# Two selective-scan layers on one core: the step products move from GpSimd to VectorE, the second output projection is cut into pieces inside the next image's loop, and TensorE adds products of zeros

## The reference

```
xc = silu(conv3x3(x @ W_in))
xs = the points of xc in 4 orders, forward and backward          # 8 scans in layer 0
delta = softplus(dt @ W_dt + b);   A = -exp(A_log)
h = exp(delta * A) * h + (delta * u) * B;   y = sum_n h_n * C_n   # for each point, state n = 0..15
y = layer_norm(sum over scans) * silu(z);   out = y @ W_out
```

## Time and profile before

| | |
|---|---|
| median of 3 runs | 15351.98 us (15345.07 to 15356.31) |
| the profiled execution, its own time | 15355.73 us |
| its span | 15353.9 us |
| granted clock over the span | 0.898 |
| VectorE busy | 13974.8 us, 91% |
| GpSimd busy | 13679.9 us, 89% |
| TensorE busy | 11962.6 us, 78% |
| ScalarE busy | 10343.2 us, 67% |

### The profile page before, as it was taken

How to read it: one execution, slowest core, us unless ns; L and a number is a source line. 1 busy time by engine, 2 the same in 40 slices (tenths; PEclk the granted TensorE clock), 3 DMA queues, 4 the chain that set the end, 5 groups by cost and what they waited for, 6 DMA issues and landing times.

```text
span 15353.9 us, 137291 instructions
## 1 busy us (share of the span) xinstructions
PE 11962.6 (78%) x45056; PEld 6538.9 (43%) x45056; DVE 13974.8 (91%) x8019; ACT 10343.2 (67%) x14003; POOL 13679.9 (89%) x5828
## 2 busy tenths in 40 slices
PE   6777877778777787777877778777787777877778
PEld 4543345433444334443345433444334443345433
DVE  8998989989899899998999989999898998989988
ACT  5666766667666676666766667666676666766667
POOL 7997989979899798997889978899789997899978
PEclk8898988989889898898988989889898898988989
DMA  5662256622566225662256622666226662266622
GB/s 188 213 214 95 88 188 215 213 93 85 193 214 215 90 82 196 215 215 86 82 201 213 216 85 80 204 215 214 84 77 209 215 214 81 77 212 214 213 76 76
DMA packets 687758, 2440.08 MB, mean 159 GB/s; under 512 B 78268, under 2 KB 100040, under 8 KB 687048
## 3 DMA queue, kind: packets, MB, share of 16 engines
q1 hardware_dynamic: 687048, 2431.29, 46.6%
HBM read 2415.26 MB, written 15.73 MB: 158 GB/s over the span
## 4 chain that ended last, share of the span: by engine, by line
POOL 48%; issue 18%; DMA 11%; DVE 10%; PE 10%; ACT 3%; POOLq 0%; DVEq 0%; SPq 0%; ACTq 0%
POOL room L1186 26%; DMA room<-bc_rows 11%; POOL room L1229 7%; POOL room L1195 4%; POOL room L1232 4%; POOL room L1221 4%; DVE room L1420 4%; PE bank L720 3%; POOL room L1176 2%; PE bank L454 2%; DVE room L1355 2%; DVE u L1312 1%; DVE room L1440 1%; DVE room L1429 1%; PE bank L792 1%
## 5 line engine op out<-in xcount | busy, mean ns | idle before, releaser
L1355 DVE TENSOR_TENSOR_SCAN room<-bank,room 128x1024 f32<-128x1024 f32 x3072 | 6903.6, 2275 | 327.5 <-issue 170.2
L1186 POOL TENSOR_TENSOR room<-room 128x1024 f32<-128x1024 f32 x3072 | 7168.0, 2374 | 0.6
L930 ACT ACTIVATE bank<-room,a 128x1024 f32<-128x1024 f32 x3072 | 3429.7, 1127 | 1046.0 <-DVE room L1355 1031.7
L720 PE MATMUL bank<-room,identity 128*128 128x512 f32 x6144 | 3007.4, 640 | 855.5 <-DVE room L1440 733.2
L1420 DVE TENSOR_TENSOR_SCAN room<-bank,room 128x1024 f32<-128x1024 f32 x1536 | 3430.9, 2273 | 54.1 <-POOL room L1229 32.4
L632 PE MATMUL bank<-identity,room 128*128 128x128 f32 x19456 | 2818.1, 295 | 4.3 <-DVE room L1363 4.1
L632 PEld LDWEIGHTS bank<-identity,room 128*128 128x128 f32 x19456 | 2525.1, 154 | 524.6 <-issue 315.6
L1363 DVE TENSOR_TENSOR room<-room,bank 128x1024 f32<-128x1024 f32 x1728 | 2071.7, 1199 | 406.1 <-PE bank L584 403.0
L720 PEld LDWEIGHTS bank<-room,identity 128*128 128x128 f32 x6144 | 1200.5, 203 | 2663.4 <-issue 1270.3
L1229 POOL TENSOR_TENSOR room<-room 128x1024 f32<-128x1024 f32 x768 | 2225.5, 2921 | 56.2 <-ACT room L1051 26.7
L584 PE MATMUL bank<-parts,pick_row 96*128 96x512 bf16 x3456 | 1245.9, 421 | 718.2 <-DVE room L1363 451.4
(11 more groups left out here) (133 smaller groups left out, 11560.2 us busy)
## 6 DMA issues: line engine op xcount, KB each, us to landing
room<-bc_rows SPq DMA_DIRECT2D x4544, 512.0 KB, 4.6
wx<-in_w_x SPq DMA_DIRECT2D x65, 162.0 KB
bc_rows<-xdbl SPq DMA_DIRECT2D x72, 128.0 KB, 4.7
pictures<-in_x SPq DMA_DIRECT2D x8, 768.0 KB, 9.0
out_x<-pictures SPq DMA_DIRECT2D x8, 768.0 KB, 7.7
weights<-in_w_in SPq DMA_DIRECT2D x16, 288.0 KB, 6.7
room<-in_w_in SPq DMA_DIRECT2D x16, 288.0 KB, 5.8
room<-in_w_out SPq DMA_DIRECT2D x16, 288.0 KB, 6.2
```

The source lines that it names most:

```text
L720: ins = nc.tensor.matmul(dst, identity[:, :], rhs, start=(q == 0), stop=(q == Q - 1))
L930: nc.scalar.activation(whole(DECAY0[g % 2]), delta0[:, j, :], ACT.Exp, scale=a0[:, col:col + 1]).then_inc(S["decay"], note("decay", (i, j, ...
L1186: nc.gpsimd.tensor_tensor(source0[:, g % SOURCES, :], du0[:, (i * J + j) % 2, :], b_ring0[:, g % BROWS, :], ALU.mult).then_inc(S["source"] ...
L1355: nc.vector.tensor_tensor_scan(run(state0[:, g % STATES, :]), run(whole(DECAY0[g % 2])), run(source0[:, g % SOURCES, :]), 0.0, ALU.mult, A ...
```

## The change

Five things. (1) `du` of layer 0 leaves GpSimd and becomes two instructions on VectorE: part 0 after the scan of n = 5, part 1 after the scan of n = 7, both for the next pass; the first pass of an image gets both halves before its first scan. Layer 1's `du1` stays on GpSimd. (2) Layer 1's output projection leaves `tail1` (but for the last image) and stands in four pieces in iterations 0, 1, 3 and 4 of the next image's `scans0`, behind that iteration's own work; both halves c now go through YACC one after the other. ScalarE takes them in iterations 4 and 6 instead of 1 and 2, VectorE adds them in iterations 5 and 9 instead of 3, and the results have a place of their own in `o2[1]`. (3) The sums of an image's first pass begin in iteration 5 instead of 4, and the semaphores of these steps are counted apart (`mm1`, `ev1`). (4) The wait for the residual ahead of scan 4 goes, since `o2[1]` is no state buffer. (5) In five iterations of every pass TensorE multiplies a block of zeros with the identity, 128 columns, twice, and adds the products to the sums.

```diff
+KEPT_BUSY = (5, 7, 9, 11, 13)
+OUT1 = {0: (0, (0, 1)), 1: (0, (2,)), 3: (1, (0, 1)), 4: (1, (2,))}
...
-        o2 = room[0:CH, 18:20, :]
+        o2 = [room[0:CH, 18:20, :], room[0:CH, 7:9, :]]
...
+            def add_nothing():
+                for h in range(2):
+                    nc.tensor.matmul(bank[:, YACC + h, 0:P], zeros[:, :], identity[:, :], start=False, stop=False)
...
-                    if n == FIRST_TERM:
+                    if b > 0 and g in OUT1:
+                        out1(b - 1, *OUT1[g])
+                    if n == FIRST_TERM and i * J + j > 0 or g == FIRST_TERM + 1:
                         begin_sums(b, i, j)
                     for lag in SUMS0.get(n, (4,)):
                         if 0 <= g - lag < len(UNITS):
                             sum_states(b, g - lag)
+                    if g < len(UNITS) and n in KEPT_BUSY:
+                        add_nothing()
...
+            def out1(b, c, tiles):
+                if c == 1 and 0 in tiles:
+                    pe.wait_ge(S["ev1"], at("ev1", ("out", 1, 0), b))
+                pe.wait_ge(S["load_wout1"], at("load_wout1", 0, b))
+                for j in tiles:
+                    pe.wait_ge(S["gat"], at("gat", (1, j), b))
+                    for h in range(2):
+                        ins = nc.tensor.matmul(bank[0:CH, YACC + h, :], wout[1][:, j, c * CH:(c + 1) * CH],
+                                               y[:, j, halves(h)], start=(j == 0), stop=(j == J - 1))
...
-                    if g in (1, 2) and b > 0:
-                        take_out1(b - 1, g - 1)
+                    if g in (4, 6) and b > 0:
+                        take_out1(b - 1, int(g == 6))
...
             def scans0(b):          # GpSimd
-                du(b, 0, 0, 0)
                 for g in range(len(UNITS)):
                     source(b, g)
...
-                    if n == 6 and ahead < PASSES:
-                        du(b, 0, ahead // J, ahead % J)
...
+            def du(b, pass_, part):          # VectorE
+                i, j = pass_ // J, pass_ % J
+                dve.wait_ge(S["dl"], at("dl", (0, i, j), b))
+                nc.vector.tensor_tensor(stored(du0[:, pass_ % 2, :])[part], stored(delta0[:, j, :])[part],
+                                        lines(u[:, j, :], SCANS[i][1])[part], ALU.mult).then_inc(
+                    S["du"], note("du", (0, i, j)))
...
-                if g == 4 and b > 0:
-                    dve.wait_ge(S["res"], at("res", (1, 1), b - 1))
...
             def scans0(b):          # VectorE
+                du(b, 0, 0)
+                du(b, 0, 1)
...
-                    if g == 3 and b > 0:
-                        residual(b - 1, 1, 0)
-                        residual(b - 1, 1, 1)
+                    if g in (5, 9) and b > 0:
+                        residual(b - 1, 1, int(g == 9))
+                    if g < len(UNITS) and n in (5, 7) and i * J + j + 1 < PASSES:
+                        du(b, i * J + j + 1, int(n == 7))
```

More of the change, by code:

```diff
@@ L155 @@
     (name, 0, h) for name in ("rest", "last") for h in range(2)}
+LATE = {("out", 1, 0), ("out", 1, 1)}
 def mm(step):
-    return "mm0" if step in AHEAD else "mm"
+    return "mm0" if step in AHEAD else "mm1" if step in LATE else "mm"
 def ev(step):
-    return "ev0" if step in AHEAD else "ev"
+    return "ev0" if step in AHEAD else "ev1" if step in LATE else "ev"
 class Counts:
@@ L235, in program @@
         turning = sb("turning", [P, P])
+        zeros = sb("zeros", [P, P])
         c_turned = sb("c_turned", [P, 2, CHUNKS, N])
@@ L784, in tail1 @@
                     head0(b + 1)
[L785 to L795, removed]
+                else:
+                    for c in range(2):
+                        out1(b, c, range(J))
             pe.wait_ge(loaded, 16 * LOADS)
-            pe.wait_ge(setup, 11)
+            pe.wait_ge(setup, 12)
             free[0] = free[1] = None
@@ L1115, in take_out1 @@
             def take_out1(b, c):
-                take_pair(b, ("out", 1, c), o2[:, c, :], ((YACC, YACC + 1), WORK)[c], rows=CH)
+                take_pair(b, ("out", 1, c), o2[1][:, c, :], (YACC, YACC + 1), rows=CH)
             def tail0(b):
@@ L1123, in tail0 @@
                 for c, banks in ((0, WORK), (1, SPARE)):
-                    take_pair(b, ("out", 0, c), o2[:, c, :], banks, rows=CH)
+                    take_pair(b, ("out", 0, c), o2[0][:, c, :], banks, rows=CH)
             def tail1(b):
@@ L1166, in _, with du1 @@
         def _(pool):
[L1167 to L1176 removed]
+            def du1(b, j):
+                pool.wait_ge(S["dl"], at("dl", (1, 0, j), b))
+                pool.wait_ge(S["yinit"], at("yinit", (1, j), b))
+                nc.gpsimd.tensor_tensor(u[:, j, :], delta1[:, j, :], u[:, j, :], ALU.mult).then_inc(
+                    S["du1"], note("du1", (1, 0, j)))
             def source(b, g):
@@ L1198, in scans0 @@
             def scans0(b):
[L1199 removed]
                 for g in range(len(UNITS)):
                     source(b, g)
[L1202 removed]
                     if g >= POOL_LAG and by_pool(*UNITS[g - POOL_LAG]):
                         weigh(b, g - POOL_LAG)
[L1205 to L1207 removed]
             def scans1(b):
[L1210 removed]
+                du1(b, 0)
                 for m, (j, n) in enumerate(UNITS1):
                     if n == 0:
[L1213 removed]
+                        pool.wait_ge(S["du1"], at("du1", (1, 0, j), b))
                     kind = f"b_line{m % BROWS1}"
@@ L1545, in _ @@
                 nc.vector.tensor_copy(dst[:, :, ::-1] if odd else dst, src).then_inc(setup, 1)
-            dve.wait_ge(setup, 11)
+            nc.vector.memset(zeros[:, :], 0.0).then_inc(setup, 1)
+            dve.wait_ge(setup, 12)
             channel_stats(0, 0, 0)
```

37 lines of the change are left out of this document (13 added, 24 removed).

## The result

The changed kernel takes **15726.8 us**, median of 4 (15716.7 to 15738.1), against 15351.2 us for the kernel before, run beside it (median of 4). The ratio is 1.0245, 95% interval [1.0227, 1.0263]: 376 us slower, where I had forecast 110.

What follows compares the result with a forecast made beforehand. GpSimd paced layer 0's loop; VectorE would take over: 46.68 busy + 2.1 port + 0.4 spread = 49.18 us per pass against 48.33. 156 - 36 - 10 = +110 us gave 15460 us, range 15230 to 15650.

Steps and rivals of the forecast that it cites:

- starts, all images: Loop starts of all eight images: -10 us from du's halves on VectorE, -36 us from moving the output projection.
- Step 1, GpSimd under VectorE: Layer 0's loop: without du GpSimd's pass falls from 48.17 to 45.69 us; delayed, it stands at 46.85, no bound.
- Step 1, du's own price: Du's two 512-point instructions on VectorE: 0.68 us each, 0.58 after overlap, 1.16 us per pass.
- Step 1, waiting for the port: Du, with two SBUF inputs, waits for GpSimd's whole instructions: 2.1 us per pass, bounds 0 and 4.62.
- The books: Timing of one pass worked out from instruction spacings: du's halves wait 0.45 and 1.44 us, together 1.89.
- Of the 1.5 us of waiting for the spread I keep 0.4: VectorE's per-pass wait ahead of weighings for TensorE's spread shrinks to 0.4 us, as du gives TensorE about 1.6 us.
- Step 2, starts: Loop starts: du's halves save 1.2 us, 8 times; the first spread ahead of the projection saves 5 us per start, -36.
- at nothing: Items counted as costing nothing, among them SyncE's later store, with some 6 us hidden, else up to 2.3 us per image.
- Step 3, zeros: TensorE's zero products: 0.5 to 0.9 us, five times a pass, hidden; their clock gain counted within the 0.4 us of waiting.
- The faster one: Rival: du finds the port free, waiting 0.6 us, with TensorE costing 0.3; pass 47.58, total 15170 us; chance 0.22.
- much slower: Rival: du waits nearly 2.31 us each time, 15870 us, or zeros lose cover, 50.3 per pass, 15670 us; chance 0.14.
- the marks I had set: Expected profile signs: du rows 1.6 to 1.9 us, some sources 2.9, GpSimd idle 2, VectorE's weighing idle halved, passes 49.2.

Runs made afterwards that it cites:

- du in PSUM: Changed kernel, but each du inside the loop multiplies delta with the next decay, in PSUM, instead of u (layer 0's result differs): 15201.1 us, ratio 0.9906.
- delta in PSUM: Changed kernel with ScalarE copying the next delta into PSUM and both du halves behind weighing 5: 15281.3 us; with the store behind unit 18 too, 15233.0 us.

## Why the prediction was wrong

The direction and the mechanism held; the sum did not. Per pass, for image 2 (46.68 + 2.1 + 0.4 = 49.18 forecast; 49.29 busy + 1.26 idle = 50.56 measured):

| term | forecast | measured | where |
|---|---|---|---|
| du's own time | 1.16 | 1.26, less overlap | du in PSUM: 29.0 us in 23 passes |
| reading columns | not seen | 0.35 | delta in PSUM: 37.0 against 29.0 |
| waiting for GpSimd | 2.1 | 2.42 | changed: 92.6 against 37.0 |
| VectorE's idle time | 0.4 | 1.26 | windows above |
| starts, all images | -46 | some -11 | scans of all images, above |

Du adds 4.03 us to a pass and VectorE's busy time grows by 3.70, since instructions without a gap between them overlap a little, as two scans do.

- **Step 1, GpSimd under VectorE: right.** Forecast 45.69 busy; 45.52 without the port (1046.93 / 23), 46.59 with it.
- **Step 1, du's own price: a term left out.** I took 0.68 from work over plain lines. In half the passes the lines are columns of u, 32 points apart: 1.03 us and over. The hint stood in the earlier trace rows: du on GpSimd took 1449 ns on average, and I used the 1.24 of a start. The Trainium skill has the effect (Advanced Engine Details and Errata, section "Memory Cachelines": an access that goes to another line of SBUF each time pays); rows agree in kind, 1.03 against 0.68.
- **Step 1, waiting for the port: right, a little low.** 2.42 against 2.1, inside the bounds. The books put 0.45 and 1.44 us on the halves; the pass shown above has 0.7 and 1.6, and over all passes the two halves average 1.80 and 2.21 us. In 306 of 368 halves inside the loops GpSimd's next instruction started in the records while du ran and took longer for it.
- **Step 1, "Of the 1.5 us of waiting for the spread I keep 0.4": the step that failed,** 0.86 x 184 = 158 us of the miss of 266. (VectorE's busy time, 49.29 for 48.78, makes another 94 and the starts 35; the pass before, 48.44 over all images for 48.33, takes 20 off.) Over the 161 passes behind the first of images 2 to 8, VectorE is idle for 1.11 us per pass ahead of weighings, 1.47 before, and for 0.22 ahead of scans, 1.34 before. I let the waits go since du gives weighings 5 and 7 a longer lead. There they went: 0.41 to 0.10 and 0.45 to 0.01 us on average. But weighing 9 has no du ahead of it, and its wait rose from 0.28 to 0.79. One place where it rose, in the 4th pass of image 2, from the timelines of VectorE and TensorE (L616 is the turn of unit 8's state, L637 sums), and a window (the third number from the right is the granted clock):

```profile
2216.63 2.15 DVE L1357 TENSOR_TENSOR room<-room,u 128x512 f32<-128x512 f32 x1
...
2220.90 1.19 DVE L1383 TENSOR_TENSOR room<-room,bank 128x1024 f32<-128x1024 f32 x1
...
2222.23 1.94 PE L616 MATMUL bank<-identity,room 128*128 128x128 f32 x8 [3.43 <-DVE room L1383]
2223.97 3.62 PE L637 MATMUL bank<-room,identity 128*128 128x512 f32 x4
2227.38 0.92 PE L595 MATMUL bank<-parts,pick_row 96*128 96x512 bf16 x2
2228.41 1.22 DVE L1383 TENSOR_TENSOR room<-room,bank 128x1024 f32<-128x1024 f32 x1 [1.94 <-PE bank L595]
```

```profile
2222.00:2224.00 2.00, 1.77 (x9) 1.80 (x10) 2.00 (x2) 0.69 (x4) 2.00 (x2) 0.50 0.64 254
```

The same steps in the kernel before (L605, L626, L584, and weighing 9 without a wait):

```profile
2169.32 1.06 PE L605 MATMUL bank<-identity,room 128*128 128x128 f32 x8 [1.79 <-DVE room L1363]
2170.22 1.88 PE L626 MATMUL bank<-room,identity 128*128 128x512 f32 x4
2171.94 0.75 PE L584 MATMUL bank<-parts,pick_row 96*128 96x512 bf16 x2
2173.47 1.19 DVE L1363 TENSOR_TENSOR room<-room,bank 128x1024 f32<-128x1024 f32 x1
```

```profile
2169.00:2172.00 3.00, 2.68 (x13) 1.60 (x13) 3.00 (x3) 2.15 (x9) 3.00 (x2) 1.00 0.64 254
```

Du's second half stands ahead of weighing 7. TensorE, which waits for that weighing, was idle for 3.43 us in place of 1.79 and went on at the half clock (0.50, 1.2 GHz) in place of the full one. Turn and sums took 1.94 and 3.62 us in place of 1.06 and 1.88, and the spread came too late. Over the 161 passes the mean granted clock between weighings 7 and 9 is 0.98 before, 0.85 in the changed kernel, 0.99 with du back on GpSimd and 0.97 with one operand in PSUM, where weighing 9 waits 0.45. So the rise goes with a du that waits for the port: I had counted du's time only as a lead for TensorE, and it is idle time for TensorE too. In the last two passes of each image weighing 9 had waited for 2.1 and 3.1 us before, now for 3.4 and 3.5.

Without the port the 0.4 does not come true either: ahead of weighings VectorE waits 0.92 us per pass with one operand in PSUM and 1.06 with delta there and the store moved, and no run with du on VectorE has less. Most of the 1.5 was there to stay; the 0.4 rested on no row of a pass that VectorE paces.
- **Step 2, starts: right in size, eaten by the store.** Of -36 - 10 the -10 came; the seven later starts gave 5 and the first lost 3. The earlier weighing came too, but under "at nothing" I wrote of the store that four rows and five sources hide some 6 us; it cost GpSimd 12.3 us at this start and the kernel some 40 us in all.
- **Step 3, zeros: right in sign and small where du is dear (38 us), large where it is cheap (136).** I had them only as a part of the 0.4. In the changed kernel they brought the clock over the span from 0.892 to 0.904.
- **Rivals.** The faster one named the right condition, a du that finds the port free; with one operand in PSUM it came out at 15201, with the whole computation at 15281. Of "much slower", the case in which the 0.4 becomes 1.5 gave 50.3 and 15670 us, nearly the measured pass, but by luck: its reason was zeros without cover, and without the zeros weighings wait for 32 us more (309.7 in all).

Against the marks I had set: du rows of 1.6 to 1.9 (2.00), sources of 2.9 beside it (2.81), GpSimd idle by some 2 us (4), weighing waits halved (403 to 277), passes of 49.2 (50.6).

## What to carry to other kernels

Before work moves between VectorE and GpSimd, count its SBUF inputs: two on VectorE beside a busy GpSimd made 0.66 us into 2.0, and laying one input in PSUM, with the halves side by side, turned a loss of 376 us into a gain of 64 (113 with the store moved back). An engine that takes over the pace does not lose its waits for the third engine: keep them in the sum unless a row shows what shortens them, and ask whom its new work keeps waiting. A queue's store that waits for a step moved later takes everything behind it along; ask of each moved step which queue waits for it, and for how long its readers last.

## What the runs showed of the hardware that was not expected

- **The port is not always handed over.** By the Trainium skill (SBUF — State Buffer, section "SBUF: two separate sides") whoever starts first gets the shared pair of ports for the whole instruction. Most rows agree: 0.55 us of du behind the end of one GpSimd instruction. But 13 halves with du behind scans 6 and 10 ended only behind the fourth or fifth GpSimd instruction that ran beside them, after up to 10.7 us, and 11 halves of the changed kernel behind the second or third, after 3.66 to 5.97. What decides it stays open.
- **Lines in columns cost on both engines**: 0.68 to 1.03 us on VectorE with u in SBUF, and on GpSimd 1.28 to 1.56 in the median (du back there). The decay in PSUM, read in the same order, cost nothing: 677 ns at most.
- **0.6 us of zeros, five times a pass, moved the time by 136 us for better, and by 66 for worse one iteration later.**
